# Lane statistics and thresholds of a pre-activation convolution kernel: per-partition scalars in place of a second SBUF tensor

## The chip, the cores and the metric

The kernel runs on one core of a Trainium2 chip. The metric is the device time of one execution in microseconds (us). One core has five engines that run their own instruction streams and meet at semaphores: TensorE (PE in the profile, its weight loads PEld), VectorE (DVE), ScalarE (ACT), GpSimd (POOL) and SyncE (SP, which here only starts DMAs).

## The reference

```python
def _L0_conv_ref(X, W, beta, v, bias, stride):
    # B: five sign filters of W; alpha: least squares; W_eff = sum alpha_m B_m
    out = 0
    for n in range(N):                       # N = 3
        An = jnp.sign(jnp.clip(X + v[n], 0.0, 1.0) - 0.5)
        out = out + beta[n] * (conv(An) + sum_alpha * bias[n])
    return out

def _gn(v, G=32, eps=1e-05):                 # one group for each channel
    m = jnp.mean(g, axis=(1, 2, 4), keepdims=True)
    s = jnp.var(g, axis=(1, 2, 4), keepdims=True)
    return ((g - m) / jnp.sqrt(s + eps)).reshape(v.shape)

x = x + _L0_conv_ref(_gn(x), W, beta, v, bias, 1)      # x: (32, 56, 56, 32), W: (3, 3, 32, 32)
```

The normalisation is never applied to the data. The sign of a shifted and clipped normalised value is the sign of the raw value against a threshold, which depends on the image's and channel's mean and deviation. So each image needs its mean and variance for each channel, from these three thresholds, and then three sign maps.

## The kernel before, in words

The 32 images are handled as 16 pairs. A pair is brought in as 112 rows (2 images x 56), transposed by PE into PSUM (`x_ps`, L689), and copied by ACT into `x_ch` (L343), where the 128 partitions are 4 column groups ("lanes") x 32 channels. Everything is done in two parts f = 0 and 1 (8 and 6 blocks of columns).

For each pair q the statistics and thresholds go as follows, all on DVE except where said:

- `lane_moments` (L559): four `bn_stats` over `x_ch`; `spread_lanes` (L566, L569): two `bn_aggr` give `lane_stats`, 6 numbers in each partition (a count, a mean and a variance for each of the 2 images), and one `tensor_tensor` of 128x24 writes them at the place of the partition's own column group and zeros at the others, by multiplying with the 0/1 mask `own_group` [128, 4];
- `gather_lanes` (L697, PE): a small fp32 matmul brings the statistics of the four lanes of a channel together in PSUM; it waits for `lanes_ready`;
- `pair_moments` (L577): two `bn_aggr` give `moments`; ACT takes the root (L353);
- `invert_root` (L581), `divide_variance` (L586), `add_root` (L590): `twice_dev` = (variance + eps) / root + root; `make_thresholds` (L595): three `scalar_tensor_tensor` of 128x2, one for each of the three sign maps, give `neg_thr`; ACT waits for `thr_ready` and makes the six sign maps (L348).

The sign maps are weighed and summed into `s_even`: the high part by DVE (`hi_part` L603 and L605, `half_hi` L609, `s_even` L616), the low part by POOL (`lo_part` L306 and L310, 128x1568 in fp16) and summed by DVE (L621). SP shifts `s_even` to `s_odd` with DMAs (L206 to L208), PE convolves (L727, L730, L735), ACT scales out (L361), PE transposes back (L747) and DVE adds x (`y_nat`, L550).

The order on every engine is written out by hand in its function `step(p)`; DVE's handles pairs p (adding x), p + 2 (sign sums), p + 3 (moments, thresholds) and p + 4 (lane statistics). One step passes for each pair. Every DVE instruction that needs the result of an earlier one waits on the semaphore `vec` (`settle`). PE's `step` handles the gather of pair p + 3 ahead of the convolution of pair p + 1, and PE's queue is in order as well.

Of the kernel before, what the change touches and what calls it, by code (L numbers as in the profile page):

```python
# [7 lines left out]
ALU = mybir.AluOpType  # L8
# [5 lines left out]
N_ACT = 3  # L14
# [3 lines left out]
G = 4  # L18
# [13 lines left out]
GN_EPS = 1e-5  # L32
# [4 lines left out]
def preact_conv_kernel(nc, x, w, beta, v, bias, out):  # L37
    ctx = ExitStack()
    with ctx:
        def sb(name, shape, dt=FP32):  # L40
            return ctx.enter_context(nc.sbuf_tensor(name, shape, dt))
# [4 lines left out]
        def sem(name):  # L46
            return ctx.enter_context(nc.semaphore(name))
# [15 lines left out]
        lane_stats = [sb(f"lane_stats{i}", [128, 2, 3]) for i in range(2)]  # L63
        spread_stats = [sb(f"spread_stats{i}", [128, G, 6]) for i in range(2)]
        moments = [sb(f"moments{i}", [128, 2, 2]) for i in range(2)]
        root = sb("root", [128, 2])
        inv_root = sb("inv_root", [128, 2])
        twice_dev = sb("twice_dev", [128, 2])
        neg_thr = [sb(f"neg_thr{i}", [128, N_ACT, 2]) for i in range(2)]

        ident = sb("ident", [128, 128])
        own_group = sb("own_group", [128, G])
# [9 lines left out]
        order = sb("order", [128, 2, N_ACT])  # L82
# [38 lines left out]
        lanes_ready = sem("lanes_ready")  # L121
# [3 lines left out]
        thr_ready = sem("thr_ready")  # L125
# [45 lines left out]
        def real(q):  # L171
            return 0 <= q < PAIRS

        def half_bank(f):

            return PER_BANK[f] * ROWS

        def load_filter(eng, o):
            eng.dma_start(w_raw[C * o:C * (o + TAPS), :, o, :], w.rearrange("a k i o -> (k i) a o"))\
                .then_inc(w_loaded, 16)  # L180
# [147 lines left out]
        @block.scalar  # L328
        def _(act):
            load_filter(act, 1)  # L330
            act.dma_start(params[:, 1, :], v.partition_broadcast(128)).then_inc(params_loaded, 16)
            act.dma_start(params[:, 0, :], beta.partition_broadcast(128)).then_inc(params_loaded, 16)
            act.dma_start(params[:, 2, :], bias.partition_broadcast(128)).then_inc(bias_loaded, 16)

            def copy_in(q, f):
                k = 2 * q + f
                n = half_bank(f)
                at = HALF_BLOCKS[f].start * ROWS
                to = x_ch[q % CH_SLOTS][:].rearrange("p i a h -> p (i a h)")[:, at:at + 2 * n]
                if f == 0 and real(q - CH_SLOTS):  # L340
                    act.wait_ge(signed, 6 * (q - CH_SLOTS + 1))
                act.wait_ge(x_transposed, k + 1)
                act.activation(to.rearrange("p (b n) -> p b n", b=2), x_ps[:, :, 0:n],  # L343
                               ACT.Copy).then_inc(x_copied, 1)

            def sign(q, n):
                for a in range(2):
                    act.activation(signs[q % 2][:, n, :, a, :], x_ch[q % CH_SLOTS][:, :, a, :], ACT.Sign,  # L348
                                   bias=neg_thr[q % 2][:, n, a:a + 1]).then_inc(signed, 1)

            def take_root(q):
                act.wait_ge(moments_ready, 2 * (q + 1))
                act.activation(root[:], moments[q % 2][:, :, 1], ACT.Sqrt, bias=eps_col[:]).then_inc(root_ready, 1)  # L353

            def scale_out(p, f):
                k = 2 * p + f
                n = half_bank(f)
                act.wait_ge(conv_done, k + 1)
                if real(p - 1):
                    act.wait_ge(y_transposed, k - 1)  # L360
                act.activation(y_ch[f][:].rearrange("p (b n) -> p b n", b=2), conv_ps[f][:, :, 0:n], ACT.Copy,  # L361
                               scale=y_scale[:]).then_inc(y_scaled, 1)

            def begin_signs(q):
                act.wait_ge(thr_ready, 3 * (q + 1))
                if real(q - 2):
                    act.wait_ge(hi_made, q - 1)
                    act.wait_ge(lo_weighed, 2 * (q - 1))
                sign(q, 1)

            def sign_filter(m):
                act.wait_ge(w_bias_ready, m + 1)
                act.activation(filt[:, :, :, :, m], w_raw[:], ACT.Sign, bias=w_bias[:, m:m + 1]).then_inc(w_signed, 1)

            def step(p):
                if real(p + 2):
                    sign(p + 2, 2)
                if real(p):
                    scale_out(p, 1)
                if real(p + 2):  # L380
                    sign(p + 2, 0)
                if real(p + 3):
                    take_root(p + 3)
                if real(p + LEAD):
                    copy_in(p + LEAD, 0)
                if p == -1:
                    copy_in(p + LEAD, 1)
                    begin_signs(p + 3)
                    act.wait_ge(y_scale_ready, 1)
                if real(p + 1):  # L390
                    scale_out(p + 1, 0)
                if p != -1:
                    if real(p + LEAD):
                        copy_in(p + LEAD, 1)
                    if real(p + 3):
                        begin_signs(p + 3)

            act.wait_ge(w_var_ready, 1)
            act.activation(w_stat[:, 5:6], w_stat[:, 4:5], ACT.Sqrt).then_inc(w_root_ready, 1)
            for m in range(3):  # L400
                sign_filter(m)
            copy_in(0, 0)
            for m in range(3, M_FIL):
                sign_filter(m)
            copy_in(0, 1)
            act.wait_ge(consts_ready, 1)
            take_root(0)
            copy_in(1, 0)
            copy_in(1, 1)
            begin_signs(0)  # L410
            for p in range(-2, PAIRS):
                step(p)

        @block.vector
        def _(dve):
            done = {"n": 0}

            def mark(ins):
                ins.then_inc(vec, 1)
                done["n"] += 1  # L420
                return done["n"]

            def settle(n=None):
                dve.wait_ge(vec, done["n"] if n is None else n)
# [5 lines left out]
            tt, ts, stt = nc.vector.tensor_tensor, nc.vector.tensor_scalar, nc.vector.scalar_tensor_tensor  # L430
# [131 lines left out]
            def spread_lanes(q):  # L562
                b = q % 2
                settle()
                for a in range(2):
                    mark(nc.vector.bn_aggr(lane_stats[b][:, a, 1:3],  # L566
                                           raw_stats[b][:, a].rearrange("p i s -> p (i s)")))
                settle()
                tt(spread_stats[b][:], own_group[:].unsqueeze(2).broadcast_to([128, G, 6]),  # L569
                   lane_stats[b][:].rearrange("p a s -> p (a s)").unsqueeze(1).broadcast_to([128, G, 6]),  # L570
                   ALU.mult).then_inc(lanes_ready, 1)

            def pair_moments(q):
                dve.wait_ge(gathered, q + 1)
# [8 lines left out]
            def divide_variance(q, n):  # L583
                dve.wait_ge(moments_ready, 2 * (q + 1))
                settle(n)
                return mark(stt(twice_dev[:], moments[q % 2][:, :, 1], GN_EPS, inv_root[:], ALU.add, ALU.mult))  # L586

            def add_root(n):
                settle(n)
                return mark(tt(twice_dev[:], twice_dev[:], root[:], ALU.add))  # L590

            def make_thresholds(q, n):
                settle(n)
                for m in range(N_ACT):
                    stt(neg_thr[q % 2][:, m, :], twice_dev[:], order[:, 1, m:m + 1], moments[q % 2][:, :, 0],  # L595
                        ALU.mult, ALU.subtract).then_inc(thr_ready, 1)

            def thresholds(q):
                make_thresholds(q, add_root(divide_variance(q, invert_root(q))))
# [51 lines left out]
            lane_moments(0, 0)  # L651
            lane_moments(0, 1)
            spread_lanes(0)
            filter_gram()
            pair_moments(0)
# [9 lines left out]
            eliminate(2)  # L665
            lane_moments(1, 1)
            spread_lanes(1)
            eliminate(3)
            eliminate(4)
# [7 lines left out]
        def _(pe):  # L677
# [13 lines left out]
                last.then_inc(x_transposed, 1)  # L691

            def gather_lanes(q):
                pe.wait_ge(lanes_ready, q + 1)
                if q:
                    pe.wait_ge(moments_ready, 2 * q)
                nc.tensor.matmul(stat_ps, same_ch[:].rearrange("p g c -> p (g c)"),  # L697
                                 spread_stats[q % 2][:].rearrange("p g s -> p (g s)"),
                                 start=True, stop=True).then_inc(gathered, 1)
# [118 lines left out]
```

## Time and profile before

| | |
|---|---|
| time, median of 3 runs (lowest, highest) | 203.67 us (201.5, 204.37) |
| profiled execution: its own time | 203.54 us |
| its span, from the first instruction to the last | 201.8 us |
| busy in the span: PE / PEld / DVE | 169.1 us (84%) / 131.4 (65%) / 171.9 (85%) |
| busy in the span: ACT / POOL | 140.7 us (70%) / 62.9 (31%) |
| mean granted clock of PE | 0.948 |

The page of the profile lists 422 DVE instructions. Busy time is counted from an instruction's start to its end, and DVE instructions that follow each other overlap a little, so the distance from start to start says what one costs in a full queue. The steps can be told apart by the one `spread_stats` of each.

### The profile page before, as it was taken

What the parts mean: (1) busy time and instruction counts of PE and PEld (TensorE: products, weight loads), DVE (VectorE), ACT (ScalarE), POOL (GpSimd) and SP (SyncE); (2) the same over time, 40 slices, a digit from 0 to 9 for tenths busy, and PEclk for the clock granted to TensorE, in tenths of its full rate; (3) what the DMA queues carried; (4) which work ended last, traced back from release to release, by engine and by line L of the source; (5) the groups of instructions that cost most, each with busy time, mean ns of one, the idle gap of its engine ahead of it and who ended that gap; (6) DMA issues with size and microseconds to landing.
All of it is one profiled execution on the core that took longest, in us unless ns stands there. A gap on an engine that the chain in (4) does not pass through costs nothing.

```text
span 201.8 us, 4766 instructions
## 1 busy us (share of the span) xinstructions
PE 169.1 (84%) x1800; PEld 131.4 (65%) x1800; DVE 171.9 (85%) x422; ACT 140.7 (70%) x183; POOL 62.9 (31%) x76
## 2 busy tenths in 40 slices
PE   1484176499999899999898999999999998989871
PEld 0383074286868587868686877776868685757560
DVE  4369999998999999999999899999999999785132
ACT  2628466297979687979787889797979796853110
POOL 6175143433233314142315051414141414240000
PEclk9996559969999999999999999999999999999996
DMA  4799433062696889888788798889898565766525
GB/s 114 226 259 265 126 82 82 0 168 59 177 248 184 234 281 234 252 227 272 211 275 242 222 237 253 240 250 246 250 241 253 142 190 140 196 196 173 179 68 159
DMA packets 21030, 39.61 MB, mean 196 GB/s; under 512 B 9744, under 2 KB 9744, under 8 KB 21008
## 3 DMA queue, kind: packets, MB, share of 16 engines
q1 hardware_dynamic: 20272, 39.27, 69.5%
q8 instruction: 14, 0.23, 0.5%
q10 hardware_dynamic: 736, 0.04, 0.2%
q14 instruction: 8, 0.07, 0.1%
HBM read 13.15 MB, written 12.85 MB: 129 GB/s over the span
## 4 chain that ended last, share of the span: by engine, by line
PE 54%; DVE 16%; DMA 10%; ACT 6%; issue 5%; SPq 4%; POOL 2%; ACTq 0%; DVEq 0%
PE conv_ps L727 31%; PE y_ps L747 11%; PE x_ps L689 7%; DMA s_odd<-s_even 6%; ACT signs L348 5%; DMA params<-in_L_conv_beta 4%; DVE y_nat L550 3%; PE conv_ps L735 2%; PE conv_ps L730 2%; DVE raw_stats L559 2%; DVE s_even L621 2%; SPq L206 2%; DVE s_even L616 2%; SPq L207 1%; PE x_ps L697 1%
## 5 line engine op out<-in xcount | busy, mean ns | idle before, releaser
L727 PE MATMUL conv_ps<-s_even,w_mm 128*64 128x448 f16 (+1 forms) x576 | 105.0, 336 | 6.9 <-issue 2.8
L730 PE MATMUL conv_ps<-s_odd,w_mm 128*64 128x448 f16 (+2 forms) x576 | 105.2, 324 | 0.0
L348 ACT ACTIVATE signs<-x_ch,neg_thr 128x784 f16<-128x784 f32 x96 | 83.7, 938 | 0.8 <-DVE neg_thr L595 0.8
L727 PEld LDWEIGHTS conv_ps<-s_even,w_mm 128*64 128x64 f16 x576 | 60.8, 111 | 33.4 <-issue 11.5
L730 PEld LDWEIGHTS conv_ps<-s_odd,w_mm 128*64 128x64 f16 x576 | 60.8, 111 | 0.1
L550 DVE SCALAR_TENSOR_TENSOR y_nat<-y_ps,y_const,x_nat 112x1024 f32<-112x1024 f32 (+1 forms) x32 | 36.7, 1146 | 11.9 <-PE y_ps L747 11.7
L306 POOL TENSOR_SCALAR lo_part<-signs,ratio_lo 128x1568 f16<-128x1568 f16 x16 | 25.6, 1597 | 63.1 <-ACT signs L348 63.0
L689 PE MATMUL x_ps<-ident,x_nat 112*128 112x112 f32 x224 | 31.0, 285 | 13.8 <-ACT x_ch L343 11.4
L310 POOL TENSOR_SCALAR lo_part<-signs,ratio_lo 128x1568 f16<-128x1568 f16 x16 | 26.7, 1666 | 40.5 <-DVE half_hi L609 22.7
L361 ACT ACTIVATE y_ch<-conv_ps,y_scale 128x896 f32<-128x896 f32 (+1 forms) x32 | 28.9, 904 | 14.8 <-PE conv_ps L730 9.7
L689 PEld LDWEIGHTS x_ps<-ident,x_nat 112*128 112x128 f32 x224 | 26.3, 157 | 15.3 <-issue 13.6
L559 DVE BATCH_NORM_STATS2 raw_stats<-x_ch 128x6 f32<-128x448 f32 (+1 forms) x64 | 31.6, 554 | 4.1 <-ACT x_ch L343 4.1
L747 PE MATMUL y_ps<-ident,y_ch 128*112 128x128 f32 x224 | 31.2, 279 | 1.5 <-DVE y_nat L550 1.5
L343 ACT ACTIVATE x_ch<-x_ps 128x896 f32<-128x896 f32 (+1 forms) x32 | 26.1, 816 | 7.0 <-PE x_ps L689 6.6
L747 PEld LDWEIGHTS y_ps<-ident,y_ch 128*112 128x112 f32 x224 | 23.4, 133 | 9.2 <-issue 7.2
L353 ACT ACTIVATE root<-moments,eps_col 128x2 f32<-128x2 f32 x16 | 4.7, 296 | 26.9 <-DVE moments L577 26.9
L735 PE MATMUL conv_ps<-s_odd,w_edge 128*64 128x112 f16 x144 | 23.4, 218 | 0.0
L616 DVE TENSOR_TENSOR s_even<-half_hi,signs 128x1568 f16<-128x1568 f16 x16 | 19.6, 1226 | 0.0
L735 PEld LDWEIGHTS conv_ps<-s_odd,w_edge 128*64 128x64 f16 x144 | 16.1, 112 | 0.0
L609 DVE TENSOR_TENSOR half_hi<-hi_part 128x1568 f16<-128x1568 f16 x16 | 15.6, 976 | 0.5
L621 DVE TENSOR_TENSOR s_even<-lo_part 128x1568 f16<-128x1568 f16 x16 | 15.5, 969 | 0.0
L605 DVE TENSOR_SCALAR hi_part<-signs,ratio_hi 128x1568 f16<-128x1568 f16 x16 | 10.1, 632 | 1.4 <-ACT signs L348 1.4
(106 smaller groups left out, 93.3 us busy)
## 6 DMA issues: line engine op xcount, KB each, us to landing
x_nat<-in_x SPq DMA_DIRECT2D x16, 448.0 KB, 5.5
out<-y_nat SPq DMA_DIRECT2D x16, 448.0 KB, 4.3
s_odd<-s_even SPq DMA_DIRECT2D x32, 203.0 KB, 3.1
s_odd<-s_even SPq DMA_DIRECT2D x32, 188.5 KB, 3.0
x_nat<-in_x SPq DMA_DIRECT2D x16, 336.0 KB, 4.9
out<-y_nat SPq DMA_DIRECT2D x16, 322.0 KB, 2.7
s_odd<-s_even SPq DMA_DIRECT2D x32, 14.5 KB, 2.8
x_nat<-in_x SPq DMA_DIRECT2D x16, 14.0 KB, 5.7
```

Of the source, the lines that this page charges most:

```text
L306: ts(lo_part[0][:], signs[q % 2][:, 1].rearrange("p i a h -> p (i a h)"), ratio_lo[:, 0:1], 1.0, ALU.mult, ALU.mult).then_inc(lo_weighed, 1)
L310: ts(lo_part[1][:], signs[q % 2][:, 2].rearrange("p i a h -> p (i a h)"), ratio_lo[:, 1:2], 1.0, ALU.mult, ALU.mult).then_inc(lo_weighed, 1)
L343: act.activation(to.rearrange("p (b n) -> p b n", b=2), x_ps[:, :, 0:n], ACT.Copy).then_inc(x_copied, 1)
L348: act.activation(signs[q % 2][:, n, :, a, :], x_ch[q % CH_SLOTS][:, :, a, :], ACT.Sign, bias=neg_thr[q % 2][:, n, a:a + 1]).then_inc(signe ...
L361: act.activation(y_ch[f][:].rearrange("p (b n) -> p b n", b=2), conv_ps[f][:, :, 0:n], ACT.Copy, scale=y_scale[:]).then_inc(y_scaled, 1)
L550: stt(y_nat[b][:, at:at + 2 * n].rearrange("p (b n) -> p b n", b=2), y_ps[0:ROWS, :, 0:n], y_const[0:ROWS, :], x_nat[p % X_SLOTS][:, C + a ...
L559: mark(nc.vector.bn_stats(raw_stats[q % 2][:, a, f, :], x_ch[q % CH_SLOTS][:, i.start:i.stop, a, :]))
L689: last = nc.tensor.transpose(x_ps[:, j // PER_BANK[f], at:at + ROWS], x_nat[s][:, 128 * i:128 * (i + 1)], ident[0:ROWS, 0:ROWS])
L727: last = nc.tensor.matmul(low[:, 0:n * ROWS], wt, s_even[b][:, part, r0:r0 + 2 * n, t:t + H], start=first, stop=end)
L730: last = nc.tensor.matmul(high[:, 0:m * ROWS], wt, s_odd[b][:, part, r0:r0 + 2 * m, t:t + H], start=first, stop=end and not at_edge)
L735: last = nc.tensor.matmul(high[:, m * ROWS:n * ROWS], we, s_odd[b][:, part, r0 + 2 * m:r0 + 2 * n, t:t + H], start=False, stop=end)
L747: last = nc.tensor.transpose(y_ps[0:ROWS, j // PER_BANK[f], at:at + 128], y_ch[f][:, j * ROWS:(j + 1) * ROWS], ident[:])
```

## The change

The write of `spread_stats` becomes four `tensor_scalar` of 128x6, one for each column group, with that group's column of `own_group` as a per-partition scalar. The thresholds are computed image by image (a = 0, 1): `divide_variance`, `add_root` and `make_thresholds` become two `tensor_scalar` each, of 128x1, 128x1 and 128x3, with `inv_root`, `root`, and `twice_dev` with the mean as per-partition scalars. The waits count the new numbers of instructions.

```diff
             def begin_signs(q):
-                act.wait_ge(thr_ready, 3 * (q + 1))
+                act.wait_ge(thr_ready, 2 * (q + 1))
...
-                tt(spread_stats[b][:], own_group[:].unsqueeze(2).broadcast_to([128, G, 6]),
-                   lane_stats[b][:].rearrange("p a s -> p (a s)").unsqueeze(1).broadcast_to([128, G, 6]),
-                   ALU.mult).then_inc(lanes_ready, 1)
+                for g in range(G):
+                    ts(spread_stats[b][:, g, :], lane_stats[b][:].rearrange("p a s -> p (a s)"),
+                       own_group[:, g:g + 1], None, ALU.mult).then_inc(lanes_ready, 1)
...
-                return mark(stt(twice_dev[:], moments[q % 2][:, :, 1], GN_EPS, inv_root[:], ALU.add, ALU.mult))
+                return [mark(ts(twice_dev[:, a:a + 1], moments[q % 2][:, a, 1:2], GN_EPS, inv_root[:, a:a + 1],
+                                ALU.add, ALU.mult)) for a in range(2)]
 
             def add_root(n):
-                settle(n)
-                return mark(tt(twice_dev[:], twice_dev[:], root[:], ALU.add))
+                for a in range(2):
+                    settle(n[a])
+                    n[a] = mark(ts(twice_dev[:, a:a + 1], twice_dev[:, a:a + 1], root[:, a:a + 1], None, ALU.add))
+                return n
 
             def make_thresholds(q, n):
-                settle(n)
-                for m in range(N_ACT):
-                    stt(neg_thr[q % 2][:, m, :], twice_dev[:], order[:, 1, m:m + 1], moments[q % 2][:, :, 0],
-                        ALU.mult, ALU.subtract).then_inc(thr_ready, 1)
+                for a in range(2):
+                    settle(n[a])
+                    ts(neg_thr[q % 2][:, :, a], order[:, 1, :], twice_dev[:, a:a + 1], moments[q % 2][:, a, 0:1],
+                       ALU.mult, ALU.subtract).then_inc(thr_ready, 1)
...
             def gather_lanes(q):
-                pe.wait_ge(lanes_ready, q + 1)
+                pe.wait_ge(lanes_ready, G * (q + 1))
```

DVE, one step in the middle of the loop, from the sum of the high part to the first product of the next step, as it was (the line numbers are those of the kernel before):

```order
L616 TENSOR_TENSOR s_even<-half_hi,signs 128x28x56
L581 RECIPROCAL inv_root<-root 128x2
L586 SCALAR_TENSOR_TENSOR twice_dev<-moments,inv_root 128x2
L590 TENSOR_TENSOR twice_dev<-twice_dev,root 128x2
L595 SCALAR_TENSOR_TENSOR neg_thr<-twice_dev,order,moments 128x2 x3
L550 SCALAR_TENSOR_TENSOR y_nat<-y_ps,y_const,x_nat 112x768
L621 TENSOR_TENSOR s_even<-lo_part 128x28x56
L559 BN_STATS raw_stats<-x_ch 128x6 x4
L566 BN_AGGR lane_stats<-raw_stats 128x2 x2
L569 TENSOR_TENSOR spread_stats<-own_group,lane_stats 128x24
L603 TENSOR_SCALAR hi_part<-signs,ratio_hi 128x1568
```

The same stretch of DVE's queue in the changed kernel (its own line numbers; those below `add_root` are 3 higher):

```order
L619 TENSOR_TENSOR s_even<-half_hi,signs 128x28x56
L581 RECIPROCAL inv_root<-root 128x2
L586 TENSOR_SCALAR twice_dev<-moments,inv_root 128x1 x2
L592 TENSOR_SCALAR twice_dev<-twice_dev,root 128x1 x2
L598 TENSOR_SCALAR neg_thr<-order,twice_dev,moments 128x3 x2
L550 SCALAR_TENSOR_TENSOR y_nat<-y_ps,y_const,x_nat 112x768
L624 TENSOR_TENSOR s_even<-lo_part 128x28x56
L559 BN_STATS raw_stats<-x_ch 128x6 x4
L566 BN_AGGR lane_stats<-raw_stats 128x2 x2
L570 TENSOR_SCALAR spread_stats<-lane_stats,own_group 128x6 x4
L606 TENSOR_SCALAR hi_part<-signs,ratio_hi 128x1568
```

Nothing moves to another place: one instruction becomes four ahead of `hi_part`, and five become six between `inv_root` and `y_nat`.

## Rows read from the trace of the kernel before

**Rows 1.** The chain that ended last, by engine (the page).

```profile
PE 54%; DVE 16%; DMA 10%; ACT 6%; issue 5%; SPq 4%; POOL 2%; ACTq 0%; DVEq 0%
```

**Rows 2.** Windows from one spread_stats to the next: busy us (instructions), PEclk, DMA.

```profile
core 0: us, PE busy (x) PEld busy (x) DVE busy (x) ACT busy (x) POOL busy (x), PEclk, DMA share, GB/s
55.31:65.59 10.28, 10.28 (x120) 8.02 (x119) 10.00 (x22) 9.08 (x13) 3.66 (x3) 1.00 0.76 218
...
137.37:147.31 9.94, 9.94 (x114) 7.45 (x113) 9.65 (x22) 8.47 (x12) 3.15 (x2) 1.00 0.89 249
...
sum 111.87, PE 108.43 PEld 83.63 DVE 107.85 ACT 94.13 POOL 35.14; mean PE 9.86 PEld 7.60 DVE 9.80 ACT 8.56 POOL 3.19
```

**Rows 3.** Timeline of DVE, one step: start us, us, what.

```profile
137.37 0.18 DVE L569 TENSOR_TENSOR spread_stats<-own_group,lane_stats 128x24 f32<-128x24 f32 x1
137.47 0.62 DVE L603 TENSOR_SCALAR hi_part<-signs,ratio_hi 128x1568 f16<-128x1568 f16 x1
...
142.39 0.16 DVE L586 SCALAR_TENSOR_TENSOR twice_dev<-moments,inv_root 128x2 f32<-128x2 f32 x1
142.59 0.16 DVE L590 TENSOR_TENSOR twice_dev<-twice_dev,root 128x2 f32<-128x2 f32 x1
142.78 0.48 DVE L595 SCALAR_TENSOR_TENSOR neg_thr<-twice_dev,order,moments 128x2 f32<-128x2 f32 x3
143.19 1.01 DVE L550 SCALAR_TENSOR_TENSOR y_nat<-y_ps,y_const,x_nat 112x768 f32<-112x768 f32 x1
...
147.31 0.18 DVE L569 TENSOR_TENSOR spread_stats<-own_group,lane_stats 128x24 f32<-128x24 f32 x1
```

**Rows 4.** Timeline of PE in that step: the gather.

```profile
137.61 0.40 PE L697 MATMUL x_ps<-spread_stats,same_ch 128*128 128x24 f32 x2
```

**Rows 5.** Line L569: all 16 (min/median/max ns), and the group's mean.

```profile
L569 DVE TENSOR_TENSOR spread_stats<-own_group,lane_stats x16: 182/183/553, 13.0 to 167.2; 128x24 f32<-128x24 f32 x16
...
L569 DVE TENSOR_TENSOR spread_stats<-own_group,lane_stats 128x24 f32<-128x24 f32 x16 | 5.0, 309 | 0.6
```

**Rows 6.** Timeline of DVE in a step with a long spread.

```profile
106.41 0.55 DVE L569 TENSOR_TENSOR spread_stats<-own_group,lane_stats 128x24 f32<-128x24 f32 x1
106.88 0.62 DVE L603 TENSOR_SCALAR hi_part<-signs,ratio_hi 128x1568 f16<-128x1568 f16 x1
```

**Rows 7.** Timeline of POOL: in that step, and in the step of Rows 3.

```profile
105.36 1.57 POOL L306 TENSOR_SCALAR lo_part<-signs,ratio_lo 128x1568 f16<-128x1568 f16 x1 [5.09 <-ACT signs L348]
...
135.68 1.57 POOL L306 TENSOR_SCALAR lo_part<-signs,ratio_lo 128x1568 f16<-128x1568 f16 x1 [4.23 <-ACT signs L348]
```

**Rows 8.** DVE's waits from 45 to 127 us: total, times, longest.

```profile
DVE y_nat L550 <- PE y_ps L747: 0.8, 2, 0.4
DVE hi_part L605 <- ACT signs L348: 0.4, 1, 0.4
```

**Rows 9.** Timeline of DVE in the fill: small instructions of other lines.

```profile
6.02 0.44 DVE L471 SCALAR_TENSOR_TENSOR w_bias<-w_stat 128x1 f32<-128x1 f32 x5
...
16.77 0.36 DVE L494 TENSOR_SCALAR neg_row<-gram,inv 128x5 f32<-128x5 f32 x1
...
17.36 0.32 DVE L494 TENSOR_SCALAR neg_row<-gram,inv 128x4 f32<-128x4 f32 x1
...
18.95 0.22 DVE L494 TENSOR_SCALAR neg_row<-gram,inv 128x3 f32<-128x3 f32 x1
19.08 0.91 DVE L559 BATCH_NORM_STATS2 raw_stats<-x_ch 128x6 f32<-128x336 f32 x2
```

**Rows 10.** Timeline of POOL at that time.

```profile
16.62 0.49 POOL L315 MEMSET filt<- 32x480 f32 x1
17.16 0.49 POOL L316 MEMSET filt<- 32x480 f32 x1
```

**Rows 11.** Timeline of DVE in the fill: the thresholds of pair 1.

```profile
26.27 1.26 DVE L586 SCALAR_TENSOR_TENSOR twice_dev<-moments,inv_root 128x2 f32<-128x2 f32 x1
...
28.16 0.97 DVE L621 TENSOR_TENSOR s_even<-lo_part 128x1568 f16<-128x1568 f16 x1
```

**Rows 12.** Timeline of POOL at that time.

```profile
25.22 2.31 POOL L310 TENSOR_SCALAR lo_part<-signs,ratio_lo 128x1568 f16<-128x1568 f16 x1 [4.35 <-DVE half_hi L609]
```

## The prediction

> **What bounds the kernel now.** I read the chain that ended last, then the windows of one step each, then DVE's own timeline. The chain names PE for 54% and DVE for 16% [rows 1], which looks like a PE-bound kernel. The windows say less than that: from the spread at 55.31 us to the one at 167.18, eleven steps take 111.87 us, 10.17 each, and PE shows busy for 9.86 and DVE for 9.80 of it [rows 2]. So I went to the timeline of one clean step, 137.37 to 147.31 us. There DVE has no wait at all: every instruction starts when the one before it allows it, for 9.94 us [rows 3]. DVE's own list of work is therefore the length of that step. PE fits into the same 9.94 us because it is held to it: its gather starts at 137.61, just behind the spread's end at 137.55 [rows 3, 4]. The chain view follows PE there because both engines arrive within a tenth of a microsecond of each other. A DVE instruction added between two spreads lengthens the step; PE only fills the gap.
>
> The seven steps before the last four take (111.87 - 4 x 9.94) / 7 = 10.30 each; the first of them, 10.28, is typical [rows 2]. They have two extras. One is contention: the spread usually takes 0.183 us but up to 0.553 [rows 5]; at 106.41 it ends at 106.96, just after POOL's lo_part, which ran from 105.36 to 106.93 [rows 6, 7]. In the clean step that lo_part ended at 137.25, 0.12 us before the spread [rows 3, 7]. All such blocking together is 16 x (0.309 - 0.183) = 2.0 us [rows 5]. The other is waiting for PE and ACT, 1.2 us in all [rows 8].
>
> **The prices.** In a full queue the cost is the distance from start to start.
> - The old spread: 0.10 us (137.37 to 137.47) [rows 3].
> - A tensor_scalar with a per-partition scalar: the nearest row is L494 at 18.95, 128x3, 0.22 us long, with the next instruction starting 0.13 later [rows 9]. The old threshold instructions, which have such a scalar too, come at (143.19 - 142.78) / 3 = 0.137 [rows 3]. I take 0.13.
> - Lower bound: five small instructions without a per-partition scalar in SBUF, L471, are over in 0.44 us. With some 0.15 for the last (as the 0.16 of L586) that is 0.07 apart [rows 3, 9].
> - Upper bound: make_thresholds now has two such scalars, which no row shows. If the second adds what the first does, 0.13 - 0.07 = 0.06, its price is 0.19.
> - A dependent instruction starts 0.04 behind the end of the one it waits for (142.39 + 0.16 to 142.59) [rows 3].
>
> **The spread, four for one.** 4 x 0.13 - 0.10 = +0.42 us a step. Bounds: 4 x 0.07 - 0.10 = +0.18, and 4 x 0.19 - 0.10 = +0.66. PE's gather is released when the fourth has ended, at 3 x 0.13 + 0.22 = 0.61 instead of 0.18, but hi_part starts later by the same amount, so PE keeps its place against DVE.
>
> **The thresholds, six for five.** Before, from L586 to y_nat: 143.19 - 142.39 = 0.80 us [rows 3]. Now the two images alternate, so each dependent instruction has a foreign one ahead of it. With 0.13 between starts the third starts at 0.26, and what it waits for ended at 0.22 and is free by 0.26: the waits are just covered. Six starts take 0.78, with the dear price for the last two 0.90. I take +0.04 a step, with ends of -0.02 and +0.10. The lower price gives pairs at 0, 0.20 and 0.40, so 0.54 in all, -0.26 a step. ACT has all thresholds after 5 x 0.13 + 0.22 = 0.87, against about 0.88 before: no change.
>
> **Gross.** Pairs 1 to 15 lie in the stretch where DVE is full: 15 x 0.46 = +6.9 us. Pair 0 lies in the fill beside POOL's sorting of beta and gives about 0.1. Together +7.0.
>
> **What comes back.** A longer DVE step gives PE and ACT room: the 1.2 us of waits should largely go [rows 8]. POOL's lo_part waits for ACT's signs; it fell onto the spread only in steps where PE, and so ACT, came late. With PE some 0.46 us less pressed, the 2.0 - 0.37 = 1.65 us of blocking outside the fill should shrink too [rows 5, 6, 7]. That is at most 2.85 us. I count 2.2, since one spread (pair 3) is blocked by a lo_part that follows DVE's own thresholds, and DMA delays won't all vanish. Net: +7.0 - 2.2 = +4.8.
>
> **Does the new form escape POOL?** The edit takes away the second SBUF tensor. Only L494 shows a small fp32 tensor_scalar beside POOL: with 3 elements it takes 0.22, with 5 and 4 it took 0.36 and 0.32 and ended at 17.13 and 17.68, as POOL's two memsets ended (17.11 and 17.65) [rows 9, 10]. So a small tensor_scalar can be held as well, even by a POOL instruction that reads nothing. I don't count on an escape for the spreads of 6 elements.
>
> The Trainium skill says the same in SBUF — State Buffer, section Who interferes with whom: a VectorE tensor_scalar can run in a two-port mode, and then takes the pair of ports it shares with GpSimd as fully as one with two SBUF inputs does, the later one waiting for the whole instruction. By that rule, which speaks against this change, the spread stays blockable; without it some 0.4 us in the fill and what is left of 1.65 us in the loop would be saved.
>
> For a single element (128x1) neither a row nor a clear rule decides. Twice in the fill L586 was held for 1.1 us until POOL's lo_part ended at 27.53 [rows 11, 12]. If its new form isn't held, little comes of it: the sum of the low part at 28.16 needs that same lo_part, so it could start at 27.6, 0.5 us earlier, twice. I leave this 0 to -1.0 us in the range.
>
> **How it stands to the runs.** The profiled execution took 203.54 us, with 201.8 of span and 1.7 around it; the median is 203.67. The forecast is 203.54 + 4.8 = 208.3. A change within 2%, about 4.1 us or up to 207.7, can hardly be told from none here. Its own range: all 2.85 back and the fill's 1.0 too, +3.1, 206.7; nothing back, 210.5; with the dear price for two scalars another 15 x 0.12 = 1.8, 212.3.
>
> **Rivals.**
> 1. *The per-partition scalar costs nothing extra in a tensor_scalar* (starts 0.07 apart). Spread +0.18, thresholds -0.26, so 15 x -0.08 = -1.2 us, and some of the 2.85 back: 199.5 to 202.3, say 201.3, faster than before. It decides from a price of about 0.08 down. For it: L471. Against it: L494 at 0.13, the same instruction with the same kind of scalar [rows 9]. In the Trainium skill, Vector Engine (DVE) Microarchitecture Reference, section 5.2, has about 75 ns for each instruction beside its elements; by that the four more instructions of a step would be 0.30 us, 4.5 us in 15 steps, and the forecast 203.54 + 4.5 - 2.2 = 205.8. The row with the scalar is dearer than that figure. Chance 0.08.
> 2. *PE or its DMAs are the true bound*, and DVE's new work goes where it waited or was blocked. Before, seven steps took 10.30 each, near 9.94 + 0.46 = 10.40. If the four clean steps had slack too, the total is +0.10 x 11 and the fill's share of about 1: 205.6. Against it: DVE has no gap in the clean steps. Chance 0.15.
> 3. *The longer spread falls on lo_part in every step.* Only 0.12 us lie between them in the clean step [rows 3, 7]. If ACT's signs move back against DVE by some 0.4, each of 11 steps is held for 0.37: +4.1 on the forecast, 212.4. Against it: ACT and PE get more room, and the new thresholds are not later. Chance 0.10.
>
> **How the numbers follow.** The forecast has 0.67. A quarter of it lies under 207.7, so slower by over 2% has 0.50 + 0.10 = 0.60; within 2%: 0.17 + 0.13 + 0.03 = 0.33; faster: 0.07. The range that leaves out about 2 in 10 runs from 205.4, rival 2, to 211.0, which takes in no recovery but not the dear price in full.
>
> **What would show it.** In the profile after: tensor_scalars of 128x6 of about 0.21 us, 0.13 apart; spread start to hi_part start 0.52; L586 to y_nat 0.78 to 0.90; steps of 10.4 us all through, with a DVE timeline without waits; spread blocked in fewer steps; PE idle ahead of the gather by 0.5 us or more; 16 x 4 = 64 more DVE instructions, 486. Wrong would be a start-to-start distance below 0.10, or steps of 10.3 and more in which DVE waits.

## The result, and the profile after

The changed kernel takes 209.63 us (median of 4 runs, 207.95 to 212.3) against 202.72 us before (median of 4, 201.5 to 204.37). The ratio is 1.0307, with a 95% interval of [1.0171, 1.0444]: slower by 3.1%, or 0.0307 x 202.72 = 6.2 us, though the interval doesn't settle that it is more than 2%. The measured time is inside the forecast's range of 205.4 to 211.0. The profiled execution, 212.3 us, is a slow run and not in the ratio; the median of the other three is 208.68 us. Some 3 us of the 212.3 are not the change's. They show in one wait of DVE near the end, first the changed kernel, then the one before:

```profile
200.10 1.02 DVE L550 SCALAR_TENSOR_TENSOR y_nat<-y_ps,y_const,x_nat 112x768 f32<-112x768 f32 x1 [7.07 <-PE y_ps L750]
191.31 1.02 DVE L550 SCALAR_TENSOR_TENSOR y_nat<-y_ps,y_const,x_nat 112x768 f32<-112x768 f32 x1 [4.06 <-PE y_ps L747]
```

Ahead of it PE waited 2.18 us for a shift DMA where it had waited 0.78, and then its granted clock was 0.50 from 196 to 198 us (the 1.2 GHz level) and 0.65 from 198 to 200, where it had been 1.00: from that wait's end to the end of `y_ps` PE took 4.9 us instead of 3.3. So I compare steps and durations, not the two spans.

The chain that ended last in the changed kernel, by engine; before it was PE 54%, DVE 16% [rows 1]:

```profile
DVE 38%; PE 30%; ACT 17%; DMA 6%; issue 6%; SPq 2%; DVEq 0%; ACTq 0%
```

Three of its windows from one spread to the next, to be held against [rows 2]:

```profile
67.76:78.22 10.46, 10.01 (x114) 7.46 (x112) 10.25 (x27) 8.47 (x12) 3.14 (x2) 1.00 0.83 238
141.08:151.55 10.47, 10.01 (x114) 7.46 (x112) 10.26 (x26) 8.47 (x12) 3.14 (x2) 1.00 0.79 224
162.01:172.48 10.47, 9.60 (x107) 6.80 (x105) 10.26 (x27) 8.61 (x12) 3.14 (x2) 1.00 0.57 161
```

The clean step went from 9.94 to 10.47 us, and from 67.76 us on nearly every step is a clean one: ten of them end at 172.48. Of the ten steps before that end at 167.18, five were of 9.94 us and five of 10.15 to 10.73. The timeline of DVE in one such step:

```profile
141.08 0.63 DVE L570 TENSOR_SCALAR spread_stats<-lane_stats,own_group 128x6 f32<-128x6 f32 x4
141.62 0.62 DVE L606 TENSOR_SCALAR hi_part<-signs,ratio_hi 128x1568 f16<-128x1568 f16 x1
...
146.54 0.33 DVE L586 TENSOR_SCALAR twice_dev<-moments,inv_root 128x1 f32<-128x1 f32 x2
146.79 0.33 DVE L592 TENSOR_SCALAR twice_dev<-twice_dev,root 128x1 f32<-128x1 f32 x2
147.04 0.48 DVE L598 TENSOR_SCALAR neg_thr<-order,twice_dev,moments 128x3 f32<-128x3 f32 x2
147.42 1.01 DVE L550 SCALAR_TENSOR_TENSOR y_nat<-y_ps,y_const,x_nat 112x768 f32<-112x768 f32 x1
```

Against [rows 3]: spread to hi_part 0.54 us instead of 0.10, L586 to y_nat 0.88 instead of 0.80. These two differences, 0.44 and 0.08, make up the 0.53 us of the step but for rounding. Where PE now stands, from the waits between 45 and 180 us (total, times, longest), with DVE's own only wait below:

```profile
PE x_ps L700 <- DVE spread_stats L570: 5.4, 10, 1.2
...
DVE y_nat L550 <- PE y_ps L750: 0.6, 1, 0.6
```

PE waits for the spread in ten steps, DVE hardly for anything.

### The profile page after: what moved, and what is told of

Same layout as the page of the kernel before. It is cut to its first block, busy times and chain, and to the rows that moved or that the text cites. A ratio compares the mean times of both kernels' runs of the same rounds, so it can differ in the third digit from the quotient of the medians.

```text
span 210.5 us, 4830 instructions
## 1 busy us (share of the span) xinstructions
PE 174.7 (83%) x1800; PEld 132.3 (63%) x1800; DVE 180.1 (86%) x486; ACT 140.2 (67%) x183; POOL 62.8 (30%) x76
## 4 chain that ended last, share of the span: by engine, by line
DVE 38%; PE 30%; ACT 17%; DMA 6%; issue 6%; SPq 2%; DVEq 0%; ACTq 0%
PE conv_ps L730 17%; ACT signs L348 14%; DVE y_nat L550 8%; DVE raw_stats L559 7%; PE y_ps L750 5%; PE x_ps L692 4%; DVE s_even L624 4%; DVE s_even L619 4%; DMA x_nat<-in_x 3%; DMA s_odd<-s_even 3%; DVE spread_stats L570 3%; ACT y_ch L361 2%; DVE neg_thr L598 2%; PE x_ps L700 1%; DVE twice_dev L586 1%
## 5 line engine op out<-in xcount | busy, mean ns | idle before, releaser
L730 PE MATMUL conv_ps<-s_even,w_mm 128*64 128x448 f16 (+1 forms) x576 | 106.6, 339 | 4.9 <-DMA s_odd<-s_even 3.0
L733 PE MATMUL conv_ps<-s_odd,w_mm 128*64 128x448 f16 (+2 forms) x576 | 106.6, 327 | 0.0
L730 PEld LDWEIGHTS conv_ps<-s_even,w_mm 128*64 128x64 f16 x576 | 61.5, 112 | 33.3 <-issue 8.7
L733 PEld LDWEIGHTS conv_ps<-s_odd,w_mm 128*64 128x64 f16 x576 | 61.5, 112 | 0.1
L692 PE MATMUL x_ps<-ident,x_nat 112*128 112x112 f32 x224 | 32.6, 295 | 13.3 <-ACT x_ch L343 10.2
L692 PEld LDWEIGHTS x_ps<-ident,x_nat 112*128 112x128 f32 x224 | 27.1, 162 | 15.5 <-issue 12.3
L700 PE MATMUL x_ps<-spread_stats,same_ch 128*128 128x24 f32 x32 | 6.6, 287 | 8.1 <-DVE spread_stats L570 7.7
```

Source lines behind the costliest of these rows:

```text
L692: last = nc.tensor.transpose(x_ps[:, j // PER_BANK[f], at:at + ROWS], x_nat[s][:, 128 * i:128 * (i + 1)], ident[0:ROWS, 0:ROWS])
L730: last = nc.tensor.matmul(low[:, 0:n * ROWS], wt, s_even[b][:, part, r0:r0 + 2 * n, t:t + H], start=first, stop=end)
L733: last = nc.tensor.matmul(high[:, 0:m * ROWS], wt, s_odd[b][:, part, r0:r0 + 2 * m, t:t + H], start=first, stop=end and not at_edge)
```

## The experiments

Each ratio is against executions of the kernel before on the same chip. "Clean step" is the distance from one spread's start to the next in the middle of the loop, read from each kernel's timeline of DVE. Unless something else is said, each started from the kernel before.

**1. The spread alone.**

```diff
-                tt(spread_stats[b][:], own_group[:].unsqueeze(2).broadcast_to([128, G, 6]),
-                   lane_stats[b][:].rearrange("p a s -> p (a s)").unsqueeze(1).broadcast_to([128, G, 6]),
-                   ALU.mult).then_inc(lanes_ready, 1)
+                for g in range(G):
+                    ts(spread_stats[b][:, g, :], lane_stats[b][:].rearrange("p a s -> p (a s)"),
+                       own_group[:, g:g + 1], None, ALU.mult).then_inc(lanes_ready, 1)
...
-                pe.wait_ge(lanes_ready, q + 1)
+                pe.wait_ge(lanes_ready, G * (q + 1))
```

> Only the spread is changed; the thresholds are as before. Full-queue theory (VectorE's starts set the step): spread to hi_part goes from 0.10 to 0.54 us, so a clean step is 9.94 + 0.44 = 10.38 us; 15 of them are 6.6, less the 2 us or so of waits and holds that the after kernel no longer had: about +4.5 us, 208. Rival (the split of the thresholds cost as much as the spread): +2.5 us or less.

Measured: 208.02 us, ratio 1.0274 [1.0214, 1.0334]. The clean step is 10.38 us (98.73 to 109.11), and between 45 and 180 us DVE has no wait that the trace lists. By the ratio that is 5.5 us, 1.0 more than expected: less came back than I had counted. The rival's +2.5 us is out.

**2. The thresholds alone** (the other half of the change's diff).

> Only the thresholds are changed. Full-queue theory: the last two instructions, with two per-partition scalars each, are 0.19 apart, L586 to y_nat 0.885 instead of 0.80, a clean step 10.02 us; 15 x 0.085 = +1.3, some of which comes back: 0 to +1.3 us. Steps with a held spread (0.55) remain, since the step is hardly longer. Rival: +2.5 us.

Measured: 203.38 us, ratio 1.0048 [1.0007, 1.0089], some 1.0 us. The clean step is 10.03 us (95.58 to 105.61). Held spreads remained, at 75.32 (0.40), 116.27 (0.55) and 126.82 us (0.55). The two halves give 1.032 together, against 1.0307 for the whole. By these two ratios more than four fifths of the loss is the spread.

**3. The old spread with four unneeded instructions behind it.**

```diff
...
                    ALU.mult).then_inc(lanes_ready, 1)
+                for g in range(G):
+                    mark(ts(spare[b][:, g, :], lane_stats[b][:].rearrange("p a s -> p (a s)"),
+                            own_group[:, g:g + 1], None, ALU.mult))
```

> The old single spread instruction and, behind it, four tensor_scalar of 128x6 with a per-partition scalar that write a tile nobody reads: work that the reference doesn't need. It parts two causes. VectorE's occupation (my theory): spread to hi_part 0.10 + 0.54 = 0.64, clean step 10.48 us, about +5.5 us in all. Rival, the later release of the gather on TensorE (0.61 instead of 0.18 us behind the start): here the gather is released as early as before, so the time stays near that of before, within 1 us.

Measured: 208.65 us, ratio 1.0326 [1.0258, 1.0395], clean step 10.47 us. That is 6.6 us, again 1.1 more than expected. The timelines of DVE and PE:

```profile
140.54 0.18 DVE L570 TENSOR_TENSOR spread_stats<-own_group,lane_stats 128x24 f32<-128x24 f32 x1
140.64 0.62 DVE L574 TENSOR_SCALAR spare<-lane_stats,own_group 128x6 f32<-128x6 f32 x4
141.18 0.62 DVE L607 TENSOR_SCALAR hi_part<-signs,ratio_hi 128x1568 f16<-128x1568 f16 x1
...
140.78 0.40 PE L701 MATMUL x_ps<-spread_stats,same_ch 128*128 128x24 f32 x2
```

The gather starts 0.24 us behind the spread, as in [rows 3, 4], and the time is lost all the same. What costs is VectorE's queue and not the later gather.

**4. The spread twice**: experiment 1 with four instructions into a tile nobody reads ahead of its four.

> The four spread instructions of the change, with four more ahead of them that write a tile nobody reads; thresholds as before. Full-queue theory: spread to hi_part 8 x 0.135 = 1.08, clean step 9.94 + 0.98 = 10.92 us; 15 x 0.98 = 14.7 less 2 to 3 that come back once: +12 us, 216. Rival, that only the first additions find VectorE the bound or that slack elsewhere absorbs them: clearly less, +8 or so.

Measured: 217.07 us, ratio 1.0734 [1.0679, 1.0789], clean step 10.91 us (91.50 to 102.41). The first four instructions, less the one that they replace, cost 0.0274 x 202.29 = 5.5 us (experiment 1), the second four (0.0734 - 0.0274) x 202.29 = 9.3. Together that is 14.8 us where 12 was expected: the 2 to 3 us that should come back did not. In 15 steps the first addition is 15 x 0.44 = 6.6 us, of which 5.5 show, so that one was partly paid out of waits and holds that it made go away. The second is 15 x 0.53 = 8.0, and more than all of it shows. The profiled executions of experiments 1 and 4 differ by 8.7 us of span: 7.4 us up to the start of the last pair's instructions, 0.5 for that pair's own four more, and 0.8 in a wait of DVE for `y_ps` behind them (1.92 against 1.16 us), the cause of which was not traced.

**5. The spread with a constant in place of the per-partition scalar** (the diff is against experiment 1).

```diff
...
-                       own_group[:, g:g + 1], None, ALU.mult).then_inc(lanes_ready, 1)
+                       0.25, None, ALU.mult).then_inc(lanes_ready, 1)
```

> Spread as four tensor_scalar of 128x6, but times a constant 0.25 instead of the per-partition mask, so the statistics of the other lanes are mixed in and the thresholds are not the reference's; thresholds as before. It prices the per-partition scalar. Theory (the scalar's read is what costs): starts 0.07 apart, 0.15 long, spread to hi_part 0.28, clean step 10.12 us, so about +2.7 less 1 to 2 that come back: +1 to +2 us. Rival (any tensor_scalar costs 0.13): as with the spread alone, +4.5 us.

Measured: 204.7 us, ratio 1.0105 [1.006, 1.0151], clean step 10.13 us. By the ratio that is 2.1 us, just above what was expected. Its group of L570 (64 instructions; min/median/max ns):

```profile
L570 DVE TENSOR_SCALAR spread_stats<-lane_stats x64: 155/164/971, 12.8 to 168.7; 128x6 f32<-128x6 f32 x64
```

The same group of the changed kernel:

```profile
L570 DVE TENSOR_SCALAR spread_stats<-lane_stats,own_group x64: 217/225/1171, 12.6 to 172.9; 128x6 f32<-128x6 f32 x64
```

The per-partition scalar takes 0.06 us in each instruction, and the distance between starts goes from 0.072 (spread to hi_part 0.29, by 4) to 0.135. Of the 0.44 us that the spread lost in a step, 0.25 go with the scalar; the rest is that there are four instructions.

**6. Two tensor_tensor for the thresholds**, in the kernel before, to take work out of DVE's queue.

```diff
-                act.wait_ge(thr_ready, 3 * (q + 1))
+                act.wait_ge(thr_ready, q + 1)
...
-                for m in range(N_ACT):
-                    stt(neg_thr[q % 2][:, m, :], twice_dev[:], order[:, 1, m:m + 1], moments[q % 2][:, :, 0],
-                        ALU.mult, ALU.subtract).then_inc(thr_ready, 1)
+                link(tt(scaled_dev[:], order[:, 1, :].unsqueeze(2).broadcast_to([128, N_ACT, 2]),
+                        twice_dev[:].unsqueeze(1).broadcast_to([128, N_ACT, 2]), ALU.mult))
+                tt(neg_thr[q % 2][:], scaled_dev[:],
+                   moments[q % 2][:, :, 0].unsqueeze(1).broadcast_to([128, N_ACT, 2]),
+                   ALU.subtract).then_inc(thr_ready, 1)
```

> Spread as before; the three threshold instructions with a per-partition scalar (3 x 0.137 = 0.41 us of VectorE's queue) become two dependent tensor_tensor of 128x6 with broadcast operands and no per-partition scalar: 0.20 + 0.08 = 0.28. Full-queue theory: a clean step is 9.94 - 0.13 = 9.81 us, 15 x 0.13 = -2.0 us against before, less if TensorE with about 9.65 us of its own work and its waits for DMAs comes into the way. Rival (PE is the bound of the clean step): no change.

Measured: 201.1 us, ratio 0.9899 [0.984, 0.9959]. That is 1% under the kernel before, the 2 us of the theory, and, by the two ratios, 4% under the changed one; these two did not run beside each other. Its DVE timeline, against the three instructions of L595, 0.48 us together, in [rows 3]:

```profile
139.99 0.17 DVE L595 TENSOR_TENSOR scaled_dev<-order,twice_dev 128x6 f32<-128x6 f32 x1
140.19 0.17 DVE L597 TENSOR_TENSOR neg_thr<-scaled_dev,moments 128x6 f32<-128x6 f32 x1
140.27 1.01 DVE L551 SCALAR_TENSOR_TENSOR y_nat<-y_ps,y_const,x_nat 112x768 f32<-112x768 f32 x1
```

139.99 to 140.27 is 0.28 us where it was 0.41, and the step is 9.82 us. In such a step (134.58 to 144.40) PE is listed busy for all of the 9.82 us, as it was for all of the 9.94 before: its busy time shrank with the step, so it did not bound the step of 9.94. The sign of the theory holds in both directions: adding to the queue lengthens the step, taking out shortens it.

**7 to 10. Does the new form escape GpSimd?** A memset on GpSimd behind its first lo_part, so that it runs when the spread comes, in the kernel before and in the changed one; first 128x640, for every pair, then 128x1280, from pair 2 on (the diff shows this one).

```diff
...
+                if q > 1:
+                    link(nc.gpsimd.memset(pool_spare[:], 0.0))
                 pool.wait_ge(signed, 6 * q + 4)
```

> The kernel before, with a memset of 128x640 on GpSimd behind each first lo_part, into a tile nobody reads, so that it runs beside VectorE's spread in every step. It shows which form is held by a GpSimd instruction that only writes. Theory: the old spread (two SBUF inputs, no two-port mode) stays at 0.18 us beside it; hi_part behind it is held instead. Rival: the old spread is held until the memset ends, as it is by lo_part.

> The changed kernel with the same memset on GpSimd behind each first lo_part. Theory: the first of the four spread instructions that meets the memset is held until it ends (the four together 0.63 us long become up to 1.2), so the new form is held by more kinds of GpSimd work than the old one. Rival (a per-partition scalar in place of the second tensor frees the instruction from GpSimd): four instructions in 0.63 us in every step. The single-element instructions of the thresholds are not held in either case.

> The kernel before with a memset of 128x1280 (about 1.27 us, twice as long) on GpSimd behind the first lo_part from pair 2 on, into a tile nobody reads. It repeats the 640-element trial, in which too little of the memset was left when the spread came. Theory: the old spread stays at 0.18 us; hi_part behind it is held until the memset ends, some 0.7 us longer than its 0.62. Rival: both are held.

> The changed kernel with the same 128x1280 memset. If a small tensor_scalar of 128x6 is held by a GpSimd instruction that only writes, the four spread instructions last until the memset ends, up to 0.9 us longer than 0.63. If it isn't (as with the short memset), they stay at 0.63 and hi_part is held in their place, by 0.4 us or so.

Measured: one execution each, 204.97 and 211.57 us with the short memset, 211.57 and 211.75 with the long one; I read only their steps. The short pair was hard to read: in the kernel before, the spread stayed at 0.18 us and hi_part took 0.76 instead of 0.62. In the changed one the four together took 0.63 us as without a memset, which looked like the rival. But the first of them alone did not. Timelines of POOL and DVE in the changed kernel with the short memset:

```profile
140.03 0.63 POOL L309 MEMSET pool_spare<- 128x640 f32 x1
...
140.33 0.36 DVE L572 TENSOR_SCALAR spread_stats<-lane_stats,own_group 128x6 f32<-128x6 f32 x1
```

It ended at 140.69, just behind the memset's 140.66, and its three followers, which start 0.13 apart in any case, hid the delay. With the long memset it is plain. The kernel before, POOL and DVE:

```profile
140.79 1.17 POOL L310 MEMSET pool_spare<- 128x1280 f32 x1
...
141.00 0.18 DVE L572 TENSOR_TENSOR spread_stats<-own_group,lane_stats 128x24 f32<-128x24 f32 x1
141.10 1.27 DVE L606 TENSOR_SCALAR hi_part<-signs,ratio_hi 128x1568 f16<-128x1568 f16 x1
```

The changed kernel, POOL and DVE:

```profile
142.15 1.17 POOL L310 MEMSET pool_spare<- 128x1280 f32 x1
...
142.39 0.97 DVE L573 TENSOR_SCALAR spread_stats<-lane_stats,own_group 128x6 f32<-128x6 f32 x4
142.93 0.84 DVE L609 TENSOR_SCALAR hi_part<-signs,ratio_hi 128x1568 f16<-128x1568 f16 x1
```

The old spread, with two SBUF tensors, passes beside an instruction that only writes, and hi_part is held in its place. The new spread is held until the memset ends (142.39 + 0.97 = 143.36, against 143.32). So the spread's new form is held by more kinds of GpSimd work than the old one, not by fewer. The Trainium skill, SBUF — State Buffer, section Who interferes with whom, has both halves of this: a VectorE instruction with two SBUF inputs contends only with GpSimd instructions that read SBUF, one in a two-port mode with all of them. The trace agrees: 0.18 us beside a memset for the one, 0.97 instead of 0.63 for the other; no run shows the mode itself. The prediction had put the two forms on a level; by the memsets they are not.

Beside a memset the starts behind the held instruction go on: hi_part started 0.54 us behind the spread as always and was held itself for the rest, 0.84 us instead of 0.62. So the long memset lengthened the changed kernel's step by 0.23 us (10.70 against 10.47), and that of the kernel before, whose hi_part met nearly all of it, by 0.68 (10.62 against 9.94).

## Why the prediction was right

**DVE's queue sets the step: shown.** All six edits to the queue moved the clean step by the distances between starts that they added or took out: 10.38, 10.03, 10.47, 10.91, 10.13 and 9.82 us, against 9.94 and the expected 10.38, 10.02, 10.48, 10.92, 10.12 and 9.81. (The prices in these expectations were by then known from the changed kernel's trace; what the experiments add is that nothing else gives way.) The third experiment excludes the gather as the cause. The second rival, PE or its DMAs as the true bound, falls with the clean steps that each addition lengthened in full and the sixth experiment shortened. Why the chain view named PE is not shown; in a clean step before, both engines filled the 9.94 us, so the view could follow either.

**The spread's price: right.** Taken 0.42 us a step, measured 0.44.

**The thresholds' price: the value taken was low, inside its bounds.** I took +0.04 with ends of -0.02 and +0.10; it is +0.085. The term that was off is the price of an instruction with two per-partition scalars: I took the middle between 0.13 and 0.19, and it is 0.19 (L598 is 0.284 us long and two of them take 0.48). The gross was therefore 15 x 0.53 = 7.9 us and not 6.9. For the same reason "no change" for ACT was wrong: the thresholds are complete 0.98 us behind the start of L586 (146.54 to 147.52) instead of 0.87. The range's "another 15 x 0.12 = 1.8" is a slip: counted from the +0.04 that was taken, the dear price adds 15 x 0.06 = 0.9, and the end is 211.4, not 212.3.

**What came back: the size about right, by another path than taken.** I took 2.2 us. By the times it is 7.9 of gross less the 6.2 measured, 1.7, with an interval far wider than the difference; between the first and the last spread of the two traces it is 2.2 (159.9 us instead of 154.2). From 67.76 us on no spread was held, and ten steps that are 0.53 us longer each took 104.7 us against 101.6 us before: 5.3 gross, 3.1 net, so 2.2 back, all that was there to come back. Ahead of that the fill gained 0.5 us twice (under "No escape from POOL"), and the holds took most of it again: they grew from 0.95 us in three spreads before (0.37, 0.22, 0.36) to 1.77. Pair 3's spread, which I had left blocked as before (0.40 us), was held much longer, since lo_part started only 0.43 us ahead of the spread and not 1.20. The POOL and DVE timelines of the changed kernel:

```profile
44.39 1.57 POOL L306 TENSOR_SCALAR lo_part<-signs,ratio_lo 128x1568 f16<-128x1568 f16 x1 [2.89 <-ACT signs L348]
...
44.82 1.56 DVE L570 TENSOR_SCALAR spread_stats<-lane_stats,own_group 128x6 f32<-128x6 f32 x4
46.30 0.61 DVE L606 TENSOR_SCALAR hi_part<-signs,ratio_hi 128x1568 f16<-128x1568 f16 x1
...
56.99 0.93 DVE L570 TENSOR_SCALAR spread_stats<-lane_stats,own_group 128x6 f32<-128x6 f32 x4
57.83 0.62 DVE L606 TENSOR_SCALAR hi_part<-signs,ratio_hi 128x1568 f16<-128x1568 f16 x1
```

Those two holds are 0.93 and 0.30 us, and here, beside a lo_part, nothing of them is hidden: hi_part starts 1.48 and 0.84 us behind the spread instead of 0.54. The trace shows why pair 3's lo_part came that late. PE's transposes ahead of ACT's copy to `x_ch` started at 40.50 us instead of 39.69, and six of them took 1.35 us instead of 0.77, at a granted clock of 0.50 (40 to 42 us, the 1.2 GHz level) instead of 1.00 (38 to 40 us); PE had stood idle for 3.1 us just before, and for 3.0 us in the kernel before. ACT's copy, its signs and lo_part followed 1.4, 1.07 and 1.06 us later than before, the spread only 0.29. So this hold is in part the clock's in this execution: with the spread alone the same spread was held for 0.16 us.

**The sum.** The forecast of +4.8 us was 1.4 short of the measured 6.2: 1.0 by the thresholds' price, the rest by the smaller recovery in the times. That 208.3 still lies 0.4 us under 208.68 is partly luck, since it started from a profiled execution of 203.54 us, 0.8 above the median of the kernel before.

**No escape from POOL: right for six elements, and the open case of one element is answered.** In the fill, beside POOL's lo_part (the first row), the changed kernel shows:

```profile
26.14 2.31 POOL L310 TENSOR_SCALAR lo_part<-signs,ratio_lo 128x1568 f16<-128x1568 f16 x1 [4.73 <-DVE half_hi L612]
...
27.19 0.33 DVE L586 TENSOR_SCALAR twice_dev<-moments,inv_root 128x1 f32<-128x1 f32 x2
27.44 0.33 DVE L592 TENSOR_SCALAR twice_dev<-twice_dev,root 128x1 f32<-128x1 f32 x2
27.69 0.96 DVE L598 TENSOR_SCALAR neg_thr<-order,twice_dev,moments 128x3 f32<-128x3 f32 x2
```

The single-element instructions pass, where L586 of before was held for 1.1 us [rows 11, 12]; the first of the 128x3 ones is held until lo_part ends at 28.45. The gain is bounded as forecast, since the low part's sum needs the same lo_part: it follows at 28.56, some 0.1 us behind lo_part's end instead of 0.6, so 0.5 us, twice.

**The rivals.** A free per-partition scalar (rival 1) is excluded by the fifth experiment: 0.06 us each. The figure of about 75 ns for each instruction, in the Trainium skill, Vector Engine (DVE) Microarchitecture Reference, section 5.2, agrees with the constant form (0.29 / 4 = 0.072 between starts) and not with that of the per-partition form (0.135). Rival 3, a hold in every step, did not come: the lo_part ends at 140.87 in the step that starts its spread at 141.08, 0.21 us apart and more than the 0.12 of before.

## What to carry to other kernels

When an in-order queue shows no gap over a whole step, the distances between its starts add up to the step's length, whatever the chain view names; test it by adding a few unneeded instructions and by taking some out. Price small instructions by the distance from start to start, and count the per-partition scalars in each: here 0.07 us with none, 0.135 with one, 0.19 with two. An addition is cheaper than its price only as long as waits and holds are left to absorb it: the first 0.44 us a step (6.6 in 15 steps) cost 5.5 us, the next 0.53 (8.0) cost 9.3.

## What the runs showed of the hardware

- A small tensor_scalar (128x6 fp32) was held by a GpSimd memset that reads nothing (0.36 us instead of 0.23 beside the short one), while a tensor_tensor with two SBUF inputs was not (0.18 us). I had expected that from two rows of the fill alone.
- A tensor_scalar of one element in each partition, with one per-partition scalar, was not held by GpSimd's lo_part (0.21 us); one of three elements with two such scalars was (0.78 instead of 0.28).
- What a hold costs depended on the GpSimd instruction. Beside a memset the instructions behind the held one started on time, and the 0.13 us hold beside the short memset left hi_part's start where it was. Beside lo_part they did not: holds of 0.93 and 0.30 us put hi_part off by 0.94 and 0.30.
